# One product of the blocked inverse moved ahead of a state product in TensorE's hand-written order (gated delta rule, one core)

## The reference

```
S = exp(g) * S + b * (outer(v, k) - outer(S k, k))
o = S q
```

## Time and profile before

| what | value |
| --- | --- |
| time, median of three runs | 1837.35 us (1837.28 to 1839.6) |
| the profiled execution's own time | 1840.0 us |
| its span, first to last instruction | 1838.2 us |
| mean granted TensorE clock | 0.948 |
| busy: PE, DVE, POOL, ACT | 1586.9, 1209.4, 957.5, 811.1 us |

### The profile page before, as it was taken

How to read it: one execution, slowest core, us unless ns; L and a number is a source line. 1 busy time by engine, 2 the same in 40 slices (tenths; PEclk the granted TensorE clock), 3 DMA queues, 4 the chain that set the end, 5 groups by cost and what they waited for, 6 DMA issues and landing times. The chain is left out here.

```text
span 1838.2 us, 75886 instructions
## 1 busy us (share of the span) xinstructions
PE 1586.9 (86%) x32268; PEld 1184.1 (64%) x32268; DVE 1209.4 (66%) x3029; ACT 811.1 (44%) x1898; POOL 957.5 (52%) x1197
## 2 busy tenths in 40 slices
PE   7579999999999999999999999659999994889950
PEld 6235666666666666666666666648888883878840
DVE  1478888888889889889888888315555552222214
ACT  1355565665565665566566556211111110333313
POOL 0145545545445545544554554205777775677853
PEclk9789999999999999999999999769999997999985
DMA  6345565665656665665665664434555541798557
GB/s 271 96 97 111 120 132 112 133 135 116 132 119 134 132 132 124 135 138 129 131 128 126 121 131 101 98 102 150 165 160 165 160 141 35 214 252 221 92 97 238
DMA packets 565041, 253.97 MB, mean 138 GB/s; under 512 B 458320, under 2 KB 532688, under 8 KB 563808
## 3 DMA queue, kind: packets, MB, share of 16 engines
q1 hardware_dynamic: 412640, 209.15, 44.2%
q10 hardware_dynamic: 133632, 20.98, 6.3%
q0 software_dynamic: 18432, 18.99, 5.9%
HBM read 177.68 MB, written 71.37 MB: 135 GB/s over the span
## 5 line engine op out<-in xcount | busy, mean ns | idle before, releaser
L376 PE MATMUL delta_p_j<-delta_xt,delta_w 128*128 128x512 f32 x768 | 387.3, 629 | 24.7 <-DMA delta_xt<-in_xt 18.6
L595 DVE SCALAR_TENSOR_TENSOR delta_kq<-delta_hist,cw,delta_kq 128x512 f32<-128x512 f32 x384 | 289.9, 755 | 30.2 <-ACT delta_kq L747 23.1
L912 POOL TENSOR_TENSOR delta_sd<-state,eg_end 128x256 f32<-128x256 f32 x128 | 129.5, 1012 | 247.5 <-DVE state L677 247.4
L1273 POOL DMA_INDIRECT slot_tokens<-mix_tokens,mix_slot x192 | 189.9, 989 | 65.4 <-issue 61.1
L740 ACT ACTIVATE delta_hist<-delta_p_j 128x512 f32<-128x512 f32 x192 | 114.1, 594 | 248.4 <-PE delta_p_j L376 224.0
L376 PEld LDWEIGHTS delta_p_j<-delta_xt,delta_w 128*128 128x128 f32 x768 | 133.3, 193 | 135.9 <-issue 121.1
L881 POOL TENSOR_SCALAR delta_n<-delta_n 128x8 f32<-128x8 f32 x64 | 15.4, 241 | 276.1 <-DVE delta_n L626 276.1
L796 ACT ACTIVATE delta_kpv<-delta_kpv,delta_root 128x64 f32<-128x64 f32 x512 | 135.5, 341 | 16.3 <-ACT delta_xit L782 16.3
L1367 PE MATMUL expert_p_h<-expert_xbt,w 128*88 128x128 f32 x1024 | 126.4, 277 | 13.2 <-ACT expert_xbt L1410 12.6
L1396 DVE SCALAR_TENSOR_TENSOR expert_gate<-expert_gate,expert_p_h 88x256 f32<-88x256 f32 x64 | 26.7, 417 | 168.4 <-ACT expert_gate L1416 112.6
L1367 PEld LDWEIGHTS expert_p_h<-expert_xbt,w 128*88 128x88 f32 x1024 | 115.9, 158 | 29.9 <-ACT expert_xbt L1410 27.2
(11 more groups left out here) (147 smaller groups left out, 3596.9 us busy)
## 6 DMA issues: line engine op xcount, KB each, us to landing
delta_xd<-x_scratch SPq DMA_DIRECT2D x256, 128.0 KB
delta_w<-in_wqkv SPq DMA_DIRECT2D x64, 416.0 KB
w<-in_w SPq DMA_DIRECT2D x64, 352.0 KB
delta_eg<-eg_rows SPq DMA_DIRECT2D x128, 130.0 KB
n_scratch<-delta_kkq ACTq DMA_DIRECT2D x128, 128.0 KB
mix_ot<-ot SPq DMA_DIRECT2D x16, 1024.0 KB
w<-in_w SPq DMA_DIRECT2D x64, 176.0 KB
delta_xd<-x_scratch SPq DMA_DIRECT2D x128, 64.0 KB
```

The lines of the kernel that those rows point to most:

```text
L376: mm = pe.matmul(view(p_j, 512 if n == 2 else 0, (1, 512)), w[e][:, (ch * 3 + n) * 128:(ch * 3 + n) * 128 + 128], xt[m // 8 % 2][:, ch * 5 ...
L595: ve.scalar_tensor_tensor(out, view(hist[e], i * 2 * 518 + tap, (259, 2), (1, 256)), cw[:, column:column + 1], out, ALU.mult, ALU.add).the ...
L912: po.tensor_tensor(view(sd, 0, (128, 2), (C, 2), (1, C)), view(state, first_pair(group) * 128, (C, 2), (128, 2), (1, C)), view(s.eg_end, g ...
L1273: po.indirect_dma_start(out=s.tok.ap(), out_offset=bass.IndirectOffsetOnAxis(ap=slot[i % 2][:, k:k + 1], axis=0), in_=tokens[:, i:i + 1], ...
```

## The change

On PE, `inverse_r` of the slot's macro is issued before `chain_state(two)` and no longer behind it. The instructions, their operands and their waits are the same, and the orders of all other engines are as they were.

```
                 if is_macro(before):
                     turn_values(before, (2, 3))
+                if is_macro(mi):
+                    inverse_r(mi)
                 if two_:
                     chain_state(*two_)
-                if is_macro(mi):
-                    inverse_r(mi)
                 if is_macro(m):
                     project(m, 1, proj_v)
```

## The result

The changed kernel takes 1850.24 us (median of 8 runs, 1843.21 to 1852.74) against 1837.51 us of the kernel before in the same session (8 runs, 1837.07 to 1842.46). The ratio is 1.0056 with an interval of 1.0038 to 1.0074: slower by 7 to 14 us, 10.3 us by the ratio itself; the two medians lie 12.7 us apart. The forecast was 1845.2 us, in a range of 1838 to 1853.

A forecast was written before the change was run, and what follows sets the result against it. PE was taken to set the pace, with DVE at 88% close behind. Main stretch +7.5 us and drain +0.3 us made +7.8 us on a median of 1837.35: 1845.2 us, range 1838 to 1853.

The forecast's parts named there:

- Odd slots, residual(two) later: DVE's residual(two) in odd slots starts later, 1.18 us on average; 0.40 us of it reaches PE's L472.
- the pair 31/32: One of fourteen slot pairs forecast to pay 0.32 to 0.78 us each; this one was put at 0.57 us.
- Even slots, no gain: L441 fills PE's 0.38 us state wait at L488 (slot 48), but PE then waits at L472: no gain alone.
- The slack before update(two): DVE's wait before update(two), 0.73 + 0.08 us in slot 51, taken as real slack that absorbs lateness.
- the prediction's rule: Per slot pair: lateness of residual(two), less DVE's three slacks, less the even slot's slack; sum over 28 pairs +7.5 us.
- The forecast's own band: Whole kernel slower by +3.7 to +11 us, 1841 to 1848.5 us; chance 0.60.
- third rival: Delay passes from pair to pair because kb slips along with DVE: +13 us, 1850 to 1853 us; chance 0.15.
- The drain: Slots after the main stretch: +0.4 us in slot 67, at most -0.1 us in even slots, together +0.3 us.
- DVE's idle time: DVE's waits swallow all the added lateness: 1835.5 to 1838.4 us, no measurable change; chance 0.13.
- PE's stalls: New waits at L472 let PE's instruction supply run ahead, so stalls vanish: faster, 1833 us at 12 us gained; chance 0.07.
- The clock: More PE idle time lowers the granted clock in the main stretch, some 3 us a drop: 1848 to 1855 us; chance 0.05.
- crossings of blocks of 256 instructions: Skill's instruction-fetch rule applied to PE's stalls inside L441, ten times, 6.2 us; crossings are mostly but not always hidden.

## Why the prediction was right, and what was mis-sized

**Odd slots, residual(two) later: right, in mechanism and size.** 0.97 us for 0.91 in slot 31; the difference is the handover from L441 to L488 and to L376, 0.06 us longer. L472 came 0.62 us later there for a forecast of 0.57. (In the sum the pair 31/32 stood at 0.57 without the 0.14 us for which slot 32 waits at L472; the sum hardly moves by it.) Odd slots alone carry the cost, and DVE's lateness alone makes it with PE's order as before.

**Even slots, no gain: right.** The state wait vanished and PE waited instead at L472, 0.31 us in most even slots. They did become 0.25 us shorter on average, 7 us together, more than the 1.8 us of filled waits. The new order in them isn't the reason: with odd slots alone changed the even slots, in the old order, take 16.80 us as well, and with even slots alone changed they take 17.17. What an odd slot is late by, the even slot behind it has in part as slack.

**The slack before update(two): the term that was mis-sized.** I took 0.73 + 0.08 us of slack there in slot 51 at face value and let the v convolution behind it keep its 1.77 us. The wait was real, but it was also what kept L609 clear of L894; with `update(two)` on time behind `horner`, L609 meets L894 and takes 2.38 us. L894 moves with DVE, so where the two meet the tap's end moves by the whole lateness that is left behind `kb`, and the slack before `update(two)` is worth nothing. From a `residual(two)` at 920.68 the chain of 8.59 us would bring L472 to 929.27 and not to 928.71: 1.0 us late instead of 0.42. The rows to see it by were in the trace of before, L609 at 1.77 us in one slot and 2.38 us in the other. This concerns the odd slots with a wait at `update(two)`: 17 of them, 6.6 us, in the kernel before, and none in the changed one. The sum over the 28 pairs, worked again from the trace of before by the prediction's rule, gives 7 to 8 us; with the first tap ending 0.55 us behind L894 wherever they meet, it gives 13 to 15 us (an estimate; the spread is what slack the even slots are granted). By the profiles the main stretch came out at +12.0 us (+14.2 in the second profile of the changed kernel) for a forecast of +7.5, by the ratio the whole at about +10.3 us (7.0 to 13.6) for +7.8. The forecast's own band, up to +11 us or 1848.5, holds by the ratio; the median of 1850.24 us lies above it, where the prediction had put its third rival. That the wider range holds by both is in part luck, as the term that took the time upwards had not been seen.

**The drain: +0.3 us forecast, open.** 0 to 5 us by its own run.

**Rivals.** DVE's idle time did not swallow the delay: 31.8 us were added to its waits at L488 (53.5 for 21.7), those at `kb` and `mask` gave back 14.5 us, and PE's wait at L472 grew by 21.3 us. PE's stalls did not vanish: 11.6 us inside L441 for 6.2, and 0.8 at L488 for 6.0, which is the same stall met by the instruction that now stands in its place; all stalls of PE together are 17.9 us in 26 for 20.2 in 32. The clock was not the cause: in the main stretch, from slot 8 on, it fell to its lower level (1.2 GHz) for 3.4 us from 495.5 in the kernel before, where slot 26 takes 19.92 us, and not at all in the changed kernel (slot 26: 17.66 us); in the second profile it fell three times for 3.4 us. Such drops come under either order and shift a single profile by 2 or 3 us. Of the third rival, more delay from pair to pair, the size came nearest, but `kb` was not what gave way: its wait shrank to 5.2 us.

## What to carry to other kernels

Work moved in front of a short instruction that another engine waits for is paid by that engine's whole queue. So cost the reader's queue, instruction by instruction, up to the next place where the first engine waits for it. Slack read off a trace is only worth its length if nothing behind it runs longer when it is gone; compare the durations of the same instruction with and without the wait in front of it. And find what stands next in line before spending work on a wait: the removed wait at L488 came back at `kb`.

## What the runs showed that I had not expected

A DVE instruction with both inputs in SBUF (L609, 128 x 512, 0.75 us) took up to 1.36 us when it began under POOL's 1.04 us L894, and with that POOL instruction cut to 0.41 us the whole kernel was 0.5% to 0.7% faster. On POOL a small product of 128 x 8 took 0.65 us for 0.20 beside L609, and a POOL instruction that reads the result of the one before starts 0.15 us after its end, where an independent one starts without a gap.

PE's stalls have fixed places. The prediction took them for crossings of blocks of 256 instructions. With PE's records, weight loads included, numbered in their order, the stalls of slots 7 to 63 stand at the same place of a block of 256 (remainder 193 to 195) in all 14 profiles, 377 of 377; about 200 such places lie in the stretch, and 23 to 32 of them show a stall of over 0.15 us. At most one of a profile's other waits falls there. So an instruction moved in PE's order changes which instruction meets the stall, as L441 does here for L488. That the stall is the fetch itself no trace shows directly.
